# The experts' sum and the state space in one stage, in a decoder of six sublayers

## What is computed

```python
# third sublayer, its end: the shared expert's output and two routed ones, weighted
x = layernorm(x + shared(x) + w0 * routed_0(x) + w1 * routed_1(x))
# fourth sublayer
z, xBC, dt = split(x @ in_proj.T, [512, 768, 8])
xBC = silu(causal_conv4(xBC) + conv_b)        # 4 taps along time, each channel by itself
x_part, B, C = split(xBC, [512, 128, 128])
dt = softplus(dt + dt_bias)
# state[h] = state[h]*exp(A[h]*dt) + (x*dt)[h] (outer) B ;  y[h] = state[h] @ C
y = (scan(x_part, B, C, dt) + x_part * D) * silu(z)
y = y * rsqrt(mean(y*y) + eps) * norm_w
x = layernorm(x + y @ out_proj.T)
```

## Time and profile before

| | us |
|---|---|
| median of three executions | 3015.48 |
| the profiled execution, its own time | 3013.87 |
| its span, first to last instruction | 3010.7 |
| combine, from its first instruction to that of the state space stage | 107.95 |
| state space, ahead of its first scan step | 43.19 |
| state space, from its first scan step to the next stage | 470.84 |

### The profile page before, as it was taken

The page is one execution under the profiler, slowest core; times in us unless marked ns, Lnnn a source line. Parts: engine busy times, 40 slices in busy tenths (PEclk is TensorE's granted clock), DMA queues, the critical chain, the costliest instruction groups (busy, mean ns, idle before and its releaser), DMA issues. The chain is left out here.

```text
span 3010.7 us, 68328 instructions
## 1 busy us (share of the span) xinstructions
PE 2506.7 (83%) x25416; PEld 2101.6 (70%) x25416; DVE 1911.4 (63%) x3347; ACT 1434.2 (48%) x2243; POOL 1591.5 (53%) x1778
## 2 busy tenths in 40 slices
PE   5999999995799978999999802888877599996998
PEld 4676766764576757999999802777777477765897
DVE  2666666775478862436665565878887267774665
ACT  2566655653466652335555401555554255653332
POOL 3566655664354530776666583445444367763343
PEclk8899999998799996999999955989998699997999
DMA  7555655532777832246666473010000578762111
GB/s 167 128 136 142 148 130 133 137 92 67 189 201 200 206 87 84 92 157 205 205 218 223 163 211 106 19 32 21 31 28 22 145 192 219 197 157 70 53 52 46
DMA packets 253228, 384.90 MB, mean 128 GB/s; under 512 B 54624, under 2 KB 184416, under 8 KB 245472
## 3 DMA queue, kind: packets, MB, share of 16 engines
q1 hardware_dynamic: 232448, 302.85, 37.9%
q0 software_dynamic: 17376, 78.13, 7.8%
q10 hardware_dynamic: 3200, 1.05, 0.2%
HBM read 249.05 MB, written 142.08 MB: 130 GB/s over the span
## 5 line engine op out<-in xcount | busy, mean ns | idle before, releaser
L1225 ACT ACTIVATE self_probs<-self_score_ps 128x768 f32<-128x768 f32 x256 | 207.6, 811 | 216.1 <-PE self_score_ps L1127 213.1
L1433 POOL TENSOR_SCALAR_AFFINE_SELECT self_probs<-self_probs 128x512 f32<-128x512 f32 x256 | 167.7, 656 | 217.0 <-ACT self_probs L1225 214.4
L2079 POOL TENSOR_TENSOR moee_h_lo<-moee_h,moee_h_hi 128x512 fp32r<-128x512 f32 x110 | 149.8, 1362 | 208.7 <-ACT moee_h_hi L1846 207.8
L1354 DVE TENSOR_REDUCE self_neg_max<-self_max_ps 128x2 f32<-128x256 f32 x256 | 108.0, 422 | 226.5 <-PE self_max_ps L1113 225.3
L672 DVE TENSOR_REDUCE cross_neg_max<-cross_max_ps 128x4 f32<-128x1024 f32 x128 | 155.9, 1221 | 69.9 <-PE cross_max_ps L461 68.6
L1950 DVE TENSOR_TENSOR moee_in_lo<-moee_in_raw,moee_in_hi 128x2048 fp32r<-128x2048 f32 x40 | 91.7, 2293 | 134.0 <-ACT moee_in_hi L1814 102.3
L1355 DVE TENSOR_REDUCE self_neg_max<-self_max_ps 128x2 f32<-128x512 f32 x256 | 174.2, 681 | 0.0
L589 ACT ACTIVATE cross_probs<-cross_score_ps 128x1024 f32<-128x1024 f32 x128 | 131.1, 1024 | 89.3 <-PE cross_score_ps L483 89.0
L1846 ACT ACTIVATE moee_h_hi<-moee_h 128x512 fp32r<-128x512 f32 x110 | 69.6, 632 | 187.5 <-DVE moee_h L2001 187.5
L3032 POOL TENSOR_TENSOR ffn_g_lo<-ffn_g_full,ffn_g_hi 128x512 fp32r<-128x512 f32 x64 | 82.4, 1287 | 144.3 <-ACT ffn_g_hi L2933 144.3
L79 PE MATMUL moee_g_ps<-moee_x_hi,moee_in_hi 128*128 128x256 f32 x440 | 131.9, 300 | 25.3 <-DVE moee_x_lo L1989 21.1
(11 more groups left out here) (475 smaller groups left out, 9932.2 us busy)
## 6 DMA issues: line engine op xcount, KB each, us to landing
self_q<-self_q_split SPq DMA_DIRECT2D x48, 512.0 KB, 3.2
self_q_raw<-self_q SPq DMA_DIRECT2D x32, 768.0 KB, 7.8
cross_stacks<-cross_qk SPq DMA_DIRECT2D x64, 384.0 KB, 6.9
causal_stacks<-causal_qk SPq DMA_DIRECT2D x64, 384.0 KB, 7.2
moe_y_tiles<-moee_y SPq DMA_DIRECT2D x55, 256.0 KB, 3.2
x_tiles<-zeros SPq DMA_DIRECT2D x16, 624.0 KB, 4.6
moee_x_t<-x_tiles SPq DMA_DIRECT2D x39, 256.0 KB, 3.2
cross_qk<-cross_k_split SPq DMA_DIRECT2D x16, 512.0 KB
```

The source lines that it names most:

```text
L1225: nc.scalar.activation(probs[g % 4][:, a, :, P:], score_ps[:, :, P:], ACT.Exp, scale=HD ** -0.5).then_inc(prob_ready, 1)
L1433: pool.affine_select(diagonal, diagonal, [[0, 2], [0, 2], [1, P]], ALU.is_ge, zero, base=0, channel_multiplier=-1).then_inc(prob_masked, 1)
L2079: pool.tensor_tensor(h_lo[p][f][:].rearrange("p j s -> p (j s)"), h[f][:], h_hi[p][f][:].bitcast(F32).rearrange("p j s -> p (j s)"), ALU.s ...
```

## The change

`combine` and its stage are gone; its work is in `state_space`, which takes `y_tiles`, the row numbers and the weights.
- **Residual in the shared tile.** Where the expert stage copied the shared result out of PSUM, it now adds x to it. So `x_res` of the combine stage is not loaded.
- **Sums ahead.** `sum_experts(b)` runs on VectorE, two batches in each odd step, five and six batches ahead of the scan; `gather(b)` on GpSimd, one batch per step, seven ahead. The sum stays in one of eight buffers `x[b % 8]`, is normalised there, and is used for the projection and for the residual. `mid[1]` of before is neither stored nor loaded.
- **Norms on ScalarE.** Both norms end as two Identity activations with scale `rstd` and bias `-mean * rstd`; GpSimd makes `rstd` and, with one more small multiply, the bias; VectorE negates the mean.
- **Pairs.** Projection, first tap, taps, Silu and the time steps work on two batches at once: eleven units per pair (B, C, x0 to x2 in the even step; dt, x3, z0 to z3 in the odd step), of one chunk and 512 columns. The taps are one operation instead of two, in place in `bc` and `xs`.
- **In place.** `decay` and `yd` are gone: the exponentials are written into `mat` and multiplied there, the D term goes into `yz` and is gated there. The low part of y is made in step n, no longer in step n+1.
- **Order.** All steps are written out (n = -7 to 16), with this order on each engine:

```diff
-        combine(nc, stage + "c", x_in, x_out, y_tiles, slot, weight, swdge[5:8])
+        state_space(nc, "ssm", y_tiles, slot, weight, swdge[5:8], x_out, ...)
...
-                        dve.tensor_copy(y[p][:].rearrange("p q d -> p (q d)"), y_ps[p][:]).then_inc(y_kept, 1)
+                        if shared(st, -2):
+                            c = QT * st.at(-2)
+                            kept = dve.tensor_tensor(y[p][:], y_ps[p][:].rearrange("p (q d) -> p q d", d=D),
+                                                     x_tok[:, c:c + QT, :], ALU.add)
...
+            # TensorE
+            for n in STEPS:
+                if now:
+                    state_products(n)
+                    exponents(n, 0)
+                    exponents(n, 1)
+                project(n, 0)
+                if late:
+                    square_sums(n - 1)
+                if now:
+                    exponents(n, 2)
+                    exponents(n, 3)
+                project(n, 1)
+                if now:
+                    exponents(n, 4)
+                    exponents(n, 5)
+                if late:
+                    output(n - 1)
+                project(n, 2)
+                if even:
+                    if real(n + 1):
+                        to_rows(n + 1)
+                    project(n, 3)
+                if now:
+                    mix(n, 0)
+                project(n, 4 if even else 3)
+                if now:
+                    mix(n, 1)
+                if not even:
+                    if real(n + 1):
+                        to_rows(n + 1)
+                    project(n, 4)
+                if real(n + 4):
+                    transpose_x(n + 4)
+                if not even:
+                    project(n, 5)
...
+            def sum_experts(b):
+                p, i = b % 3, b % 8
+                dve.wait_ge(sh_loaded[p], (b // 3 + 1) * 16)
+                dve.wait_ge(routed_loaded[p], (b // 3 + 1) * TOP * QT * 16)
+                for q in range(QT):
+                    c = b * QT + q
+                    dve.scalar_tensor_tensor(y_shared[p][:, q, :], y_routed[p][:, 0, q, :], weight[0][:, c:c + 1],
+                                             y_shared[p][:, q, :], ALU.mult, ALU.add).then_inc(part_ready, 1)
+                dve.wait_ge(part_ready, 2 * b + 2)
...
+                moments(b, x[i], c_stats, c_mv[b % 2], c_var[b % 2], c_low[b % 2], cstat_ready, cmean_ready, ceps_ready)
...
+            # VectorE
+            for n in STEPS:
+                if now:
+                    masked_products(n)
+                    tail_rows(n)
+                    matrices(dve, n, 0, low_mat_ready)
+                if even:
+                    taps(n, 0)
+                else:
+                    time_steps(n)
+                if now:
+                    matrices(dve, n, 2, low_mat_ready)
+                taps(n, 1)
+                if now:
+                    matrices(dve, n, 4, low_mat_ready)
+                if late:
+                    mean_squares(n - 1)
+                if even:
+                    taps(n, 2)
+                else:
+                    exponent_terms(n)
+                if late:
+                    residual(n - 1)
+                if soon:
+                    high_terms(n + 1)
+                if even:
+                    scaled_rows(n + 1), taps(n, 3), skip_terms(n, 0), taps(n, 4)
+                else:
+                    sum_experts(n + 5), skip_terms(n, 0)
+                skip_terms(n, 1), gated(n)
+                if not even:
+                    scaled_rows(n + 1), sum_experts(n + 6)
+                # low part of x of batch n + 4
...
+            # GpSimd
+            for n in STEPS:
+                matrices 1, 3 of n; scale_rows(n - 1); matrices 5 of n
+                if even: scale_x(n + 5)
+                low_terms(n + 1); scale_y(n - 1); gather(n + 7)
+                if n == -6: split_weights()
+                split_y(n)
+                if not even: scale_x(n + 5)
...
+            # ScalarE: even: tails, decays 0-1, tap B, decays 2-3, tap C, decays 4-5, normalize_x(n+4), taps x0 x1,
+            #          normalize_y(n-1), tap x2, split_x(n+4), split_y(n)
+            # odd: tails, decays 0-1, log_terms, decays 2-3, tap x3, decays 4-5, normalize_x(n+4), silus, z0 z1,
+            #      normalize_y(n-1), z2, split_x(n+4), split_y(n), z3
```

More of the change, by code:

```diff
@@ L2642, in _, with moments @@
-            run(dve, body)
+            def moments(b, r, stats, mv, var, low, stats_there, mean_there, eps_there):
+                for q in range(QT):
+                    dve.bn_stats(stats[:, q, :], r[:, q, :]).then_inc(stats_there, 1)
+                dve.wait_ge(stats_there, 2 * b + 2)
+                dve.memset(gate[:], 0.0)
+                for q in range(QT):
+                    dve.bn_aggr(mv[:, q, :], stats[:, q, :]).then_inc(mean_there, 1)
+                dve.wait_ge(mean_there, 2 * b + 2)
+                dve.tensor_scalar(low[:], mv[:, :, 0], -1.0, None, ALU.mult)
+                dve.tensor_scalar(var[:], mv[:, :, 1], EPS, None, ALU.add).then_inc(eps_there, 1)
@@ new lines, in mean_squares, with residual @@
+            def mean_squares(b):
+                dve.wait_ge(ssq_done, b + 1)
+                if b:
+                    dve.wait_ge(scale_ready, b)
+                dve.tensor_scalar(ms[:], g_ps[:, 448:448 + QT], 1.0 / INNER, EPS, ALU.mult, ALU.add).then_inc(ms_ready, 1)
+            def residual(b):
+                i, p = b % 8, b % 2
+                dve.wait_ge(y_done, b + 1)
+                dve.wait_ge(scale_ready, b + 1)
+                if b >= 2:
+                    dve.wait_ge(stored[p], b // 2 * 16)
+                for q in range(QT):
+                    last = dve.scalar_tensor_tensor(y_out[p][:, q, :], y_ps[0][:, q * D:(q + 1) * D],
+                                                    row_scale[:, q:q + 1], x[i][:, q, :], ALU.mult, ALU.add)
+                last.then_inc(r_ready, 1)
+                dve.wait_ge(r_ready, b + 1)
+                if b >= 2:
+                    dve.wait_ge(shift_ready, b - 1)
+                moments(b, y_out[p], stats, mv[p], var[p], low[p], stat_ready, mean_ready, eps_ready)
@@ new lines, in skip_terms @@
+            def skip_terms(n, blk):
+                if blk == 0 and n:
+                    dve.wait_ge(yhi_ready, n)
+                    dve.wait_ge(sq_ready, n)
+                    dve.wait_ge(ylo_ready, n)
+                dve.wait_ge(ssm_done, 2 * n + blk + 1)
+                for i in range(2):
+                    f = 2 * blk + i
+                    last = dve.scalar_tensor_tensor(yz[:, f, :], cols_of(xs[:, n // 2 % 2, f, :], n), dcol[:, f:f + 1],
+                                                    y_ps[blk][:, i * S:(i + 1) * S], ALU.mult, ALU.add)
+                last.then_inc(yd_ready, 1)
@@ new lines, in _ @@
+            for n in STEPS:
+                now, late, soon = real(n), real(n - 1), real(n + 1)
+                even = n % 2 == 0
+                if now:
+                    matrices(pool, n, 1, high_mat_ready)
+                    matrices(pool, n, 3, high_mat_ready)
+                if late:
+                    scale_rows(n - 1)
+                if now:
+                    matrices(pool, n, 5, high_mat_ready)
+                if even and real(n + 5):
+                    scale_x(n + 5)
+                if soon:
+                    low_terms(n + 1)
+                if late:
+                    scale_y(n - 1)
+                if real(n + 7):
+                    gather(n + 7)
+                if n == -6:
+                    split_weights()
+                if now:
+                    split_y(n)
+                if not even and real(n + 5):
+                    scale_x(n + 5)
```

881 lines of the change are left out of this document (443 added, 438 removed).

## The result

| | before | after |
|---|---|---|
| median | 3014.41 us (4 executions) | 2970.61 us (4 executions, 2968.40 to 2971.47) |
| profiled execution, its span | 3010.7 us | 2969.7 us |
| combine and head, up to the first `gm` | 151.14 us | 78.47 us |
| first `gm` to the next stage | 470.84 us | 507.21 us |
| everything else | 2388.7 us | 2384.0 us |

A forecast was written before the change was run, and what follows sets the result against it. VectorE was taken as the bound, busy 24.7 of 28.98 us per step, with waits carrying the new steps. Head -79.1 and steps -12.8 made -92: 3013.9 to 2922, as median 2923 us, range 2872 to 2962.

The forecast's parts named there:

- Head: From the stage's first instruction at 1728.4 to the first gm: gm at 1800.4 against 1879.5, -79.1 us, 8 either way.
- The even step: Even scan step on VectorE: 24.0 us own work plus waits for chunks B, C, x0 and the tail, given as 28.7.
- the clock low only for chunk B's 2.6 us: Even step: chunk B's six products start after VectorE's low part of x, run 2.6 us at lower clock; VectorE waits 1.2.
- the walk: The four engines' new orders laid side by side with traced durations: even step 28.7, odd 31.7, mean 30.2 us.
- TensorE at 1.2 GHz: Rival, chance 0.04: the clock stays low for whole steps, 21 us of TensorE work become 42; 3088 us.
- The odd step: Odd scan step on VectorE: 22.5 us own work, waits 5.2 up to the exponent terms, 2 and 2.15; 31.7 in all.
- The locks: VectorE and GpSimd excluding each other in odd steps: 2 us at the high terms, 2.15 at the second sum.
- Steps 11 and 13: Odd steps without sums of expert rows: 24 us each, 48 together.
- The end: Steps 14 and 15 without projections 35.6 us, then last norm to next stage 17.3 as before.
- The end of the norm: Norm's last operations leaving VectorE: 2.30 us less VectorE work per step.
- Gathers late: Rival, chance 0.13: gathers on GpSimd delay the low part of y and what follows, 12 steps x 3 us; 2959 us.
- Waits as now: Rival, chance 0.23: locks do not bind and TensorE runs ahead; steps take 26 to 28.2 us; 2885 us.

The follow-up runs named there:

- a_fill: Kernel after plus 18 spare 512-column products on TensorE ahead of chunk B in even steps 2 to 10; 2942.07 us.
- j_unit1_odd: Kernel after with chunk x3 projected ahead of the sums of squares in odd steps; 2951.61 us.
- f_fill_both: a_fill plus 16 spare products ahead of the dt product in odd steps 1 to 9; 2939.32 us.
- g_ylo_dve: Kernel after with the low part of y made by VectorE behind the next step's gm, instead of by GpSimd; 2942.54 us.
- k_all_moves: Kernel after with low part of y on VectorE, low part of x ahead of odd steps' second sum, second projection ahead of squares in every step; 2913.40 us.
- d_both: Kernel after with low part of x ahead of odd steps' second sum, and sums of squares behind the second pair of exponents in all steps; 2961.81 us.
- p_squares_late_odd: k_all_moves with the sums of squares behind exponents 2 and 3 in odd steps alone; 2906.44 us.
- m_norm_vector: Kernel after with the end of the second norm back on VectorE, as two tensor_scalar in place of ScalarE's Identity activations; 2978.06 us.
- q_fill9: a_fill with 9 spare products in place of 18; 2951.05 us.
- e_no_lock: Kernel after with GpSimd writing zeros as the low part of y instead of subtracting, so part of the output product is left out; 2943.37 us.

## Why the prediction was wrong, step by step

**Head: right** (78.5 us, forecast 72.0 within 8; the kernels with the early low part of x have 72.0 to 74.0).

**Steps: 507.2 us, forecast 458.** By kind, and the 49 us by step:

| | forecast | measured | miss |
|---|---|---|---|
| even steps 0 to 12 | 198.6 | 218.0 | +19.4 |
| odd steps 1 to 9 | 158.5 | 174.8 | +16.3 |
| steps 11 and 13 | 48 | 52.9 | +4.9 |
| step 14 to the next stage | 52.9 | 61.5 | +8.6 |

**The even step** failed at one term: "the clock low only for chunk B's 2.6 us". The prediction had seen that chunk B would start late, on VectorE's last operation, and had priced what it saw in the trace of before: slow products for some 3 us behind a gap of 4.68. Behind the new gap of 5.06 it was 12 us. In VectorE's waits it reads so: B 1.2 forecast and 1.85 measured, C 1.25 and 2.90, x0 2.2 and 2.85, and 1.77 for exponentials 2, which the walk had at nothing; 4.7 us more than forecast. a_fill shows the rest of the walk was sound (27.9 for 28.7 forecast), and step 12 too (27.85). The rival "TensorE at 1.2 GHz" named the mechanism; I had worked it out only for whole steps, as all or nothing, gave it 0.04, and left the middle, a third of a step, in nobody's sum. It alone is +20.5 us (five steps of 32.8 for 28.7). The written sum has a slip beside it: 24.0 of own work and waits of 1.2, 1.25, 2.2 and 0.3 make 28.95 and not 28.7, some 2 us over seven steps.

**The odd step** lacks a wait in the walk: 2.87 us for x3's first tap, behind squares at 3.54 us and exponents and products at 0.43 per 512 columns. In the walk the waits up to the exponent terms were 5.2; tail 1.07, the lock at the start 2.3, exponentials 1.67, x3 2.87 and the logarithm 0.60 make 8.5. j_unit1_odd takes 2.0 us of it away by order alone. But the walk as written prices no low clock in the odd step, and f_fill_both shows what it is worth: with 3.4 us of it in place of 10.2 the waits for exponentials 2 and x3 are 2.1 us shorter, and the step 2.4. So most of the 3.3 us missed is the same term as in the even step, left out a second time; order and clock each shorten it, and what makes the clock fall there even without a gap stays open.

**The locks** were right in sum and partly in place. Second sum: 2.11 us (2.15). The high terms ran free of one (2.35 us for two); in their stead two small operations waited, `a` at 1.27 us and the norm's variance at 1.88, together some 2.8 (forecast 2). What I had not seen is that the lock ends in TensorE's gap, and so costs a second time in the even step: of the 28 us that g_ylo_dve gains, 14.6 lie there.

**Steps 11 and 13** have the order that j_unit1_odd mends (24.7 and 24.2 for 24 forecast). **The end**: half of the 8.6 us is step 14 (22.2 us for the 17.8 of the sum), half what follows. In step 15 TensorE stands 4.28 us ahead of the squares and then runs them in 3.55; before, they came behind the exponent products, in 1.95. No run moved that: k_all_moves has 39.3 us from the last `gm` to the next stage like the kernel after. Step 14 fell to 20.1 and 20.2 us in d_both and p_squares_late_odd; its cause was not looked into.

**The end of the norm**, counted at -2.30 us, was a lock in the trace of before; without one it takes 0.72 to 0.86, and the whole move is worth 8 us by the ratios of m_norm_vector, hardly clear of noise, where 2.30 per step were counted.

**Rivals.** "Gathers late" gave 2959, the closest number, and was absent: 0.95 us each, and steps 9 and 10, without gathers, are as long (35.10 and 33.13) as 7 and 8 with them (35.06 and 33.12). "Waits as now" was absent too.

## What to carry to other kernels

If an order makes TensorE's next products depend on the last operation of the slower engine, price the low clock for a third of a step as well as for none and all, and look who waits for TensorE then: the same kind of gap cost 4.9 us a step in one kernel and 0.6 to 0.9 in the other. Fill the gap with spare products first, to see what a better order can bring; then put real work there, the products whose inputs are ready, and take what stands between the gap and its end (here a lock) away. Then look at the granted clock again: a filled gap did not always keep it up.

## What the runs showed of the hardware

- **How long the clock stays low differs.** Behind 5.06 us of idle TensorE the granted clock was 0.50 for 12 us of nearly unbroken products; behind 2.47 us (g_ylo_dve) 0.61 over 4.1 us and then 1.00; behind 4.68 us in the kernel before, some 3 us. The Trainium skill, TensorE: Matmul & The Clock Gate, section on HAM oscillation, tells that idle gaps between bursts of products send the clock down again in every round of a loop; the trace agrees, in every even step from 2 to 10. The length of the gap is not what makes the difference: behind 3.00, 3.03 and 3.04 us in q_fill9 the clock was 1.00, 0.88 and 0.61 over 11.8 us. And it fell with no gap to speak of: in step 5 of f_fill_both it was 0.50 for 10 us, with TensorE busy in 9.93 of the 10.20 us and without a pause in the 2.30 us before. What decides it is not settled by these runs.
- **The sums of squares take 3.54 us at the low clock and 1.84 at the high one** for the same 16 products of one column.
- **The lock strikes the smallest operations.** A tensor_scalar of 2 elements took 1.88 us beside GpSimd's low terms, where the one ahead of it, alike but negating, took 0.17; in the kernel after, step 7:

```profile
2049.15 0.17 DVE L2549 TENSOR_SCALAR ssm_low<-ssm_mv 128x2 f32<-128x2 f32 x1
2049.23 1.88 DVE L2550 TENSOR_SCALAR ssm_var<-ssm_mv 128x2 f32<-128x2 f32 x1
```

- **A memset on GpSimd did not lock these.** In e_no_lock it writes the same 1024 elements while VectorE's two operations take 0.87 us:

```profile
2048.76 0.87 DVE L2558 SCALAR_TENSOR_TENSOR ssm_y_shared<-ssm_y_routed,moek_weight,ssm_y_shared 128x256 f32<-128x256 f32 x2
...
2048.79 0.95 POOL L2791 MEMSET ssm_y_lo<- 128x1024 f32 x1 [1.98 <-ACT ssm_y_hi L2463]
```
